# Which queue loads the second reading of layer 0's tiles: a graph network kernel, before and after one change

## What is computed

```python
u = par_u[0] * par_u[1] * (diag_u[:, None] * ego_u @ W_u) + ego_u      # first 2048 rows
i = par_i[0] * par_i[1] * (diag_i[:, None] * ego_i @ W_i) + ego_i      # other 3072 rows
e = concatenate([u, i])
h = adj @ (adj.T @ e)
x = layernorm(x + layernorm(h) * gamma + beta + x)
# layer 1: Chebyshev terms of adj, four weights
T1 = adj @ x;  T2 = 2 * (adj @ T1) - x;  T3 = 2 * (adj @ T2) - T1
x = layernorm(x + x @ w[0] + T1 @ w[1] + T2 @ w[2] + T3 @ w[3] + bias)
```

## Time and profile before

| what | value |
|---|---|
| time, median of three runs | 1199.03 us (1196.73 to 1199.1) |
| profiled execution | 1196.89 us |
| its span, first to last instruction | 1195.1 us |
| PE busy | 1105.3 us, 92% |
| DVE busy | 920.1 us, 77% |
| ACT busy | 334.6 us, 28% |
| POOL busy | 257.6 us, 22% |
| HBM read | 338.48 MB, 284 GB/s over the span |
| SP's queue q1 | 232.11 MB |
| ACT's queue q10 | 104.87 MB |
| POOL's queue q0 | 2.86 MB |

### The profile page before, as it was taken

The page is one execution under the profiler, slowest core; times in us unless marked ns, Lnnn a source line. Parts: engine busy times, 40 slices in busy tenths (PEclk is TensorE's granted clock), DMA queues, the critical chain, the costliest instruction groups (busy, mean ns, idle before and its releaser), DMA issues.

```text
span 1195.1 us, 13907 instructions
## 1 busy us (share of the span) xinstructions
PE 1105.3 (92%) x5004; PEld 479.5 (40%) x5004; DVE 920.1 (77%) x960; ACT 334.6 (28%) x598; POOL 257.6 (22%) x420
## 2 busy tenths in 40 slices
PE   4999999999999998799889999999899999988884
PEld 3444444444445453444333333444334444422221
DVE  2698798999899899698777766655577777678783
ACT  1456546546556555400101000000110000011111
POOL 0476645555354354100000000000000000001121
PEclk9999999999999999999999999999999999989998
DMA  7999999999999995899999999999599999999980
GB/s 225 305 286 297 295 281 314 280 300 301 284 296 271 289 286 131 193 300 306 237 346 346 338 318 314 296 295 255 145 334 347 336 341 348 307 315 346 343 235 11
DMA packets 362170, 340.33 MB, mean 285 GB/s; under 512 B 11292, under 2 KB 360772, under 8 KB 362132
## 3 DMA queue, kind: packets, MB, share of 16 engines
q1 hardware_dynamic: 253812, 232.11, 69.6%
q10 hardware_dynamic: 105600, 104.87, 30.3%
q0 software_dynamic: 2720, 2.86, 1.0%
HBM read 338.48 MB, written 1.31 MB: 284 GB/s over the span
## 4 chain that ended last, share of the span: by engine, by line
PE 57%; SPq 12%; DVE 12%; ACT 10%; issue 4%; ACTq 2%; POOL 1%; DMA 1%; DVEq 0%; POOLq 0%
PE bank L1219 30%; ACT terms L803 9%; SPq L372 7%; SPq L361 5%; DVE turned L531 4%; PE bank L1232 4%; PE bank L1287 4%; PE bank L1089 2%; PE bank L1049 2%; PE bank L1077 2%; ACTq L314 2%; PE bank L1101 2%; PE bank L1061 2%; DVE shared L551 2%; PE bank L1265 1%
## 5 line engine op out<-in xcount | busy, mean ns | idle before, releaser
L1219 PE MATMUL bank<-turned,terms 128*128 128x512 f32 x664 | 294.9, 597 | 4.5 <-DVE turned L531 3.2
L421 POOL COPY raw<-raw 32x512 f32<-32x512 f32 x320 | 194.7, 609 | 243.5 <-DVE raw L568 205.7
L551 DVE STREAM_TRANSPOSE shared<-shared 32x512 f32<-32x512 f32 x320 | 224.0, 700 | 4.1
L1049 PE MATMUL bank<-shared 128*64 128x256 f32 x1600 | 206.6, 385 | 6.3 <-DMA shared<-in_adj 6.2
L531 DVE STREAM_TRANSPOSE turned<-shared 128x2048 f32<-128x2048 f32 x70 | 160.4, 2302 | 59.9 <-PE bank L1219 37.0
L531 DVE STREAM_TRANSPOSE turned<-raw 128x2048 f32<-128x2048 f32 x70 | 159.8, 2297 | 53.4 <-PE bank L1219 38.4
L803 ACT COPY terms<-terms 32x512 f32<-32x512 f32 x320 | 197.1, 616 | 5.1 <-DVE terms L561 0.9
L1219 PEld LDWEIGHTS bank<-turned,terms 128*128 128x128 f32 x664 | 123.5, 190 | 165.6 <-issue 159.2
L466 POOL DMA_DIRECT2D out<-scratch x40 | 21.7, 549 | 667.3 <-DVE scratch L759 667.2
L1049 PEld LDWEIGHTS bank<-shared 128*64 128x64 f32 x1600 | 112.4, 136 | 87.6 <-issue 33.6
L794 ACT COPY scratch<-bank 128x512 f32<-128x512 f32 x80 | 46.6, 585 | 131.1 <-PE bank L1061 130.8
(11 more groups left out here) (150 smaller groups left out, 1048.1 us busy)
## 6 DMA issues: line engine op xcount, KB each, us to landing
shared<-in_adj SPq DMA_DIRECT2D x100, 1024.0 KB, 10.8
raw<-in_adj SPq DMA_DIRECT2D x100, 512.0 KB, 10.5
raw<-in_adj ACTq DMA_DIRECT2D x100, 512.0 KB, 12.3
shared<-in_adj SPq DMA_DIRECT2D x100, 512.0 KB, 10.2
shared<-in_adj ACTq DMA_DIRECT2D x100, 512.0 KB, 12.1
raw<-in_adj SPq DMA_DIRECT2D x80, 256.0 KB, 7.7
xq<-in_x POOLq DMA_DIRECT2D x40, 32.0 KB, 6.1
out<-scratch POOLq DMA_DIRECT2D x40, 32.0 KB, 4.6
```

The costliest lines, as they stand in the source:

```text
L421: last = nc.gpsimd.tensor_copy(moved[Q32 * c:Q32 * (c + 1), :, :, Q32 * q:Q32 * (q + 1)], beside[Q32 * q:Q32 * (q + 1), :, c, :, :])
L551: last = nc.vector.transpose(low_turned[Q32 * c:Q32 * (c + 1), :, :, Q32 * q:Q32 * (q + 1)], low[Q32 * q:Q32 * (q + 1), :, :, Q32 * c:Q32 ...
L1049: last = nc.tensor.matmul(t_bank[H * odd:H * (odd + 1), 0:PW], e[:, s * SB + b, :], panels[slot][:, s * SB + b, :], start=(k == 0 and b < ...
L1219: last = nc.tensor.matmul(sum_bank[parity][:, :], terms[:, c * GB + i, columns], turned[place][:, i * BANK:(i + 1) * BANK], start=(first a ...
```

## The change

- SP: x comes in five DMAs, one for each segment, each with a semaphore of its own; the weight blocks, the parameter rows and all tile loads leave its program. After its layer 1 loads it stores the ninth output block and half of the tenth, and waits for both blocks' stores.
- ScalarE: it issues the four weight blocks and the two parameter rows at its start, and the other half of the tenth block at its end.
- GpSimd: it issues the first two tiles ahead of its first move, and tile j after move j for j from 2 to 19. It stores the first eight output blocks alone.
- VectorE and TensorE: the diagonals have a semaphore of their own and come first; VectorE waits for each piece of x. In the finish TensorE multiplies by `both` (two identities of 64 below each other), which sums the two halves, in place of a transpose, and VectorE copies the sum in one operation in place of two.

```diff
@@ sync
-            sp.dma_start(e[:, :, :], x.rearrange("(b p) f -> p b f", p=P)).then_inc(x_loaded, DMA)
-            sp.wait_ge(w_cleared, 1)
-            for k, a in enumerate((W_u, W_i)):
...
+            x_rows = x.rearrange("(b p) f -> p b f", p=P)
+            for k, s in enumerate(SEGS):
+                b = slice(s * SB, (s + 1) * SB)
+                sp.dma_start(e[:, b, :], x_rows[:, b, :]).then_inc(x_loaded[k], DMA)
...
-                    if k in (1, 3) and k // 2 < len(tiles):
-                        load_layer0_tile(*tiles[k // 2])
...
-                load_panel(0, pair - 1, end - 2 * PW, [(1, (pair - 1) * TILED - 3, end - 2 * BANK)])
-                load_panel(1, pair - 1, end - PW, [(0, (pair - 1) * TILED - TILED, end - BANK)])
-            load_layer0_tile(1, T1 - 1 - TILED, (NG - 1) * BANK)
+                load_panel(0, pair - 1, end - 2 * PW)
+                load_panel(1, pair - 1, end - PW)
...
+            for n in (NG - 2, NG - 1):
+                sp.wait_ge(out_made, n + 1)
+                for q in range(NQ if n == NG - 2 else NQ // 2):
+                    store(sp, n, q, last_stored)
+            sp.wait_ge(last_stored, DMA * NQ * 2)
@@ gpsimd
+            def load_layer0_tile(k, group):
+                if group >= 1:
+                    pool.wait_ge(tile_turned, (group - 1) * TILED + k + 1 + RAW)
+                for q in range(NQ):
+                    pool.dma_start(raw[k][Q32 * q:Q32 * (q + 1), :].rearrange("p (b c) -> p b c", c=P),
+                                   tile_rows[2 * SEGS[k] + 1][:, :, group * BANK + P * q:group * BANK + P * (q + 1)])\
+                        .then_inc(raw_loaded[k], DMA)
...
                 pool.wait_ge(beside_moved, j + 1)
+                if j >= 2 and j // 2 < NG:
+                    load_layer0_tile(j % 2, j // 2)
...
+            for k in range(TILED):
+                load_layer0_tile(k, 0)
             move_beside(1)
...
-            for n, g in enumerate(ROWS3):
+            for n in range(NG - 2):
                 pool.wait_ge(out_made, n + 1)
@@ vector
-            dve.wait_ge(consts_loaded, DMA * 8)
+            dve.wait_ge(diag_turned, 1)
+            chain(nc.vector.tensor_copy(diag[:, :], t_bank[:, 0:NB]))
+            dve.wait_ge(consts_loaded, DMA * 6)
...
-                chain(nc.vector.tensor_copy(y, halves[:, :, 0:H]))
-                nc.vector.tensor_tensor(y, halves[:, :, H:PH], y, ALU.add).then_inc(out_taken, 1)
+                nc.vector.tensor_copy(y, by_chunk(out_bank[n % 2][:, 0:GB * H], H)).then_inc(out_taken, 1)
@@ scalar
+            act.wait_ge(w_cleared, 1)
+            for k, a in enumerate((W_u, W_i)):
...
+            act.wait_ge(out_made, NG)
+            for q in range(NQ // 2, NQ):
+                store(act, NG - 1, q, last_stored)
@@ tensor
-                    last = nc.tensor.transpose(out_bank[i % 2][:, c * P:(c + 1) * P], o_turned[:, c * P:(c + 1) * P],
-                                               ident[:, :])
+                    last = nc.tensor.matmul(out_bank[i % 2][:, c * H:(c + 1) * H], o_turned[:, c * P:(c + 1) * P],
+                                            both[:, :], start=True, stop=True)
```

More of the change, by code:

```diff
@@ L155, in resnorm_chebyshev @@
         consts_loaded = sem("consts_loaded")
-        x_loaded = sem("x_loaded")
+        diag_loaded = sem("diag_loaded")
+        x_loaded = [sem(f"x_loaded{k}") for k in range(NS)]
         xq_loaded = sem("xq_loaded")
@@ L315, in load_part, with store @@
                             rows_of[:, :, at_column:at_column + SPAN * P]).then_inc(pair_loaded[u % SLOTS], DMA)
+        def store(queue, n, q, stored):
+            queue.dma_start(quarter(out, ROWS3[n], q),
+                            by_chunk(scratch[Q32 * q:Q32 * (q + 1), 2 + n % 2, 0:GB * H], H)).then_inc(stored, DMA)
         def by_chunk(a, width):
@@ L338, in _, with load_panel @@
         def _(sp):
-            sp.dma_start(diag_rows[0:UB, :], diag_u.rearrange("(b p) -> b p", p=P)).then_inc(consts_loaded, DMA)
-            sp.dma_start(diag_rows[UB:NB, :], diag_i.rearrange("(b p) -> b p", p=P)).then_inc(consts_loaded, DMA)
-            sp.dma_start(e[:, :, :], x.rearrange("(b p) f -> p b f", p=P)).then_inc(x_loaded, DMA)
-            sp.wait_ge(w_cleared, 1)
-            for k, a in enumerate((W_u, W_i)):
[L344 to L349, removed]
-            seg_rows = adj.rearrange("(s b p) c -> s p b c", p=P, b=SB)
[L354 to L365, removed]
+            sp.dma_start(diag_rows[0:UB, :], diag_u.rearrange("(b p) -> b p", p=P)).then_inc(diag_loaded, DMA)
+            sp.dma_start(diag_rows[UB:NB, :], diag_i.rearrange("(b p) -> b p", p=P)).then_inc(diag_loaded, DMA)
+            x_rows = x.rearrange("(b p) f -> p b f", p=P)
+            for k, s in enumerate(SEGS):
+                b = slice(s * SB, (s + 1) * SB)
+                sp.dma_start(e[:, b, :], x_rows[:, b, :]).then_inc(x_loaded[k], DMA)
+            seg_rows = adj.rearrange("(s b p) c -> s p b c", p=P, b=SB)
+            def load_panel(slot, uses, column, first=False):
                 for k, s in enumerate(SEGS):
@@ L778, in _ @@
         def _(act):
+            act.wait_ge(w_cleared, 1)
+            for k, a in enumerate((W_u, W_i)):
+                for half in range(2):
+                    rows_of = slice(H * half, H * (half + 1))
+                    act.dma_start(w_pair[rows_of, k, rows_of], a).then_inc(consts_loaded, DMA)
+            for k, a in enumerate((par_u, par_i)):
+                act.dma_start(par[:, 2 * k:2 * k + 2], a.rearrange("(o n) -> o n", o=1).to_broadcast([P, 2]))\
+                    .then_inc(consts_loaded, DMA)
             for n in range(NS):
```

18 lines of the change are left out of this document (8 added, 10 removed).

## The result

| | before | after |
|---|---|---|
| median of the runs, us | 1198.99 (1196.73 to 1199.1, 5 runs) | 1191.95 (1188.52 to 1192.64, 5 runs) |
| the profiled execution, us (its span) | 1196.89 (1195.1) | 1188.52 (1186.7) |
| ratio to before | | 0.9939, 95% interval 0.9923 to 0.9955 |

What follows compares the result with a forecast made beforehand. Mostly TensorE bounds the span; layer 0 is bound by SP's DMA issues to 160 us, then compute. Front -1.7 (+1.0 - 1.5 - 3.1 + 1.9) and end -8.7 give -10.4 us: 1187.5, range 1181.0 to 1196.0.

Steps and rivals of the forecast that it cites:

- Panel 0: Start of layer 0: panel 0 done 1.0 us later, at 36.8, because two tiles come ahead of or beside it.
- sum of transfers: Start, from 3.0 us: x 6.2 us, tiles 10.2, panel 0 15.1, so panel 0 is in at 34.5 us.
- The stalls: Layer 0's transfer waits go: 1.5 us at panel 1 and 3.1 us over panels 2 to 6.
- The tile issues: GpSimd in layer 0: 0.8 us per issue, four per tile, covered by the compute-bound period, costing nothing.
- rival three: GpSimd becomes the bound if a tile issue takes over 2.9 us; at 3.5 us, 1222 us total; chance 0.10.
- The last tile: End of layer 0: its load follows the 19th move, so VectorE waits 1.9 us and all behind shifts.
- The finish: Last finish loses VectorE's add and gap, -0.46 us; TensorE's product with `both` taken as costing 0.
- The stores: Program end: last stores on hardware queues and GpSimd's DRAIN covered, so last result to end falls 8.2 us.
- rival four: Program end: a 7 us DRAIN follows the last store on whichever queue, giving 1194.5 us; chance 0.10.
- One: Software and hardware queues together move tiles at the panels' rate; panel 0 3.2 us sooner, 1183.3 us; chance 0.18.
- Two: Nothing won at the front: stalls stay, last tile costs 5.4 us, total -2.3 us, 1195.6; chance 0.12.

Runs made afterwards that it cites:

- the three edits together: Changed kernel with tile 0 behind panel 0, tile 1 behind panel 1, last tile ahead of move 19, xq adds ahead of tile issues: 1180.59 us, 0.9859.
- the tiles back on SP: Changed kernel with layer 0's tiles issued by SP among the panels again, all else kept: 1185.66 us, ratio 0.9894 to the kernel before.
- the adds ahead: Changed kernel with GpSimd's two late adds on xq ahead of the tile issues: 1189.18 us, ratio 0.9937 to the kernel before.
- the old finish: Changed kernel with transposes, copy and add again instead of the product with `both`: 1190.59 us, ratio 0.9949 to the kernel before.
- the stores alone: Kernel before with only the last two groups' stores moved to SP's and ScalarE's hardware queues: 1189.08 us, ratio 0.9923.
- the tiles alone: Kernel before with only layer 0's tiles issued by GpSimd; x, constants and stores as before: 1199.80 us, ratio 1.0004.

## Why the prediction was right, and where it was off

The sum was -10.4 us. Measured were -8.4 between the profiled executions and -7.0 between the medians. The difference is in the front, which came out with the wrong sign (+3.2 for -1.7); what holds the forecast is the end. The 8.4 is helped by luck, the 2.9 us of the middle: the second profile of the same kernel was only 4.4 us under before (1192.46 against 1196.89).

*Panel 0: +1.0 forecast, bounds -3.2 to +4; +4.7 measured. This step failed.* That panel 0's end waits for transfers is right: TensorE waited 1.43 us for the last piece, in at 38.4 where the sum had 34.5. What was mis-sized is the sum of transfers. It had x and both tiles in by 19.4 us and 348 GB/s from there on; in the trace the fifth piece of x is scaled at 22.82 and 348 GB/s are reached at 24. The stretches from 3 to 24 us have 205 GB/s in the mean, 4.3 MB, which is 0.9 MB more than x and the tiles: so much of panel 0 went at the low rate. By 38.4 us 9.5 MB had moved, some 0.7 MB more than constants, x, tiles and panel 0: panel 1's first pieces shared the way, which the sum left out.

With the tiles on SP, behind panel 0, its last piece is in at 25.9 us by the trace's landings (24.3 in the sum), so the tiles ahead of it cost 12.5 us of transfer, not 10.2. At the copy only 11.0 of that is seen (40.47 less 29.46), since without tiles it is not transfers that bind but the way from x to the pass: VectorE begins its chain at 9.16 instead of 15.38, TensorE begins the pass at 20.55 and needs 8.85 us without a wait, and the rest of that way, 11.39 us, is as long as before (11.51). I had this way in the upper bound only. So the new start by itself won 6.3 us and not the 9.2 of the sum without tiles (36.8 - 10.2 = 26.6, against 35.79), and that 11.0 lies near the 10.2 forecast is in part luck.

*The stalls: -1.5 and -3.1 forecast; -1.5 and -3.1 measured.* The first period fell from 19.8 to 18.3, the five after from 113.55 to 110.47. For the five the reason given holds, SP is off the chain: with panel 0 early, in the run with the three edits together, they are 110.47 as well (50.95 to 161.42), and with the tiles back on SP 115.23 (52.21 to 167.44). For the first period the condition was not seen: its stall is gone where panel 0 is late, and comes back where panel 0 is early and a tile runs beside panel 1. With two tiles it is 26.2 us, 7.9 over the 18.3, with one 20.3 in the run with the three edits: there the bytes asked for beside a panel decide.

*The tile issues: 0.8 us forecast, 0.651 measured, worked out from the earlier trace rows.* Nothing waits for them in general, and rival three falls. But "costs nothing" was wrong in one panel: GpSimd's own next operation, the add on xq, stands behind the issues too, and met VectorE's copy: 1.4 us. The prediction named the moves behind the issues and forgot the add. The run with the adds ahead shows it.

*The last tile: +1.9 forecast, a wait of 2.13 measured.* The step is right: layer 1's first turn came 1.7 us later against the last t copy than before (29.0 against 27.3). Without the wait it was 28.9 too, since TensorE met a stretch of low clock there. Two runs show the wait alone, with the granted clock at 1.00 from 460 to 488 us: the old finish (a wait of 2.05, 28.8 us) and the changed kernel a second time (2.36, 29.2). At the full clock the wait is thus worth 1.5 to 1.9 us.

*The finish: -0.46 forecast; 0 measured.* TensorE's price was taken as nothing; it is 0.44 us (1.10 for the four chunks against 0.66 in the earlier trace rows).

*The stores: -8.2 forecast; -8.7 measured at the end of the trace, 9.2 (7.7 to 10.8) under before by the run with the stores alone.* The mechanism is the one given, and rival four falls: no DRAIN of 7 us follows stores on the hardware queues.

*The rivals.* One falls: tiles and panels together ran at 230 to 240 GB/s, below the panels' 348. The Trainium skill (DMA: Bandwidth & Descriptors, Issuing engines are not separate DMA queues) lets all queues end at the same 16 engines; the traces agree, with a tile in SP's own queue the same 230 GB/s move (tiles back on SP, 30 to 36 us). Two falls by its reasons: the stalls went and the last tile was waited for 2.1 us, not 5.4. But what it said of the front, that nothing is won there, is what came, by way of panel 0 and the add. Three falls by the issues. In the sum, the front is +3.2 to the first turn of layer 1 where -1.7 stood; that is 4.9 us, of which panel 0 has 3.7, the add 1.4, and the rest is the last tile, 0.2 less than forecast.

The rule that rival three leaned on has another side. The Trainium skill (SBUF — State Buffer, Who interferes with whom) gives the ports that GpSimd and a VectorE copy in a two-port mode share to whichever issues first, and lets the other wait for the whole instruction. By it VectorE can be the one that waits. The trace agrees: VectorE's copy ended at 235.03, GpSimd's add at 234.98, and the copy was 0.29 us in the run with the adds ahead, where the add was over. The other direction, which the prediction weighed, did not show: the median tile issue is the fastest one, 651 ns.

## What to carry to other kernels

A load moved to an idle queue is not free: it moves ahead in the order of bytes. Price it by its transfer time at the place where it now lands, and issue it behind the data that the start waits for, one load at a time; here that order alone was worth 6 to 8 us. At the end of a program look at what stands behind the last result: 8.7 of the 11.4 us there went with the software queue's last stores and its DRAIN, and that part alone was the whole gain of this change.

## What the hardware showed that was not expected

- GpSimd's closing DRAIN went with what its queue had carried: 7.012 us before, 6.359 with the last two groups' stores on other queues (the stores alone; the tiles back on SP), 3.664 with the 80 tile issues added (the tiles alone), 3.011 with both (the changed kernel and the seven other runs made from it with the tiles on GpSimd). The tile issues take 3.348 us off it in both pairs, the two groups of stores 0.653. SP's lasted 7 to 13 ns and ScalarE's 150 or 151 ns behind their stores. Why GpSimd's is shorter with more issues is open.
- Two tiles of 1.05 MB beside 1 KB pieces of panels lowered the rate of all transfers together from 348 to 230 to 240 GB/s. One tile more beside panel 1 put its last piece back by 5.3 us.
- In two profiles of the changed kernel TensorE's granted clock stood at its lower level for 13.7 and 20.5 us of layer 1 up to 1175 us, and the spans were 1186.7 and 1190.7. A change of 1 to 2 us is not to be told in medians of this kernel, only in the trace.
